# Geometric attention blocks ahead of the standard ones in each chunk of a causal two-attention layer with a ternary feed-forward

## The reference

```python
q, k = rope(xn @ Wq), rope(xn @ Wk)          # 8 query heads, 2 key heads of 32 channels
v = xn @ Wv                                   # 2 value heads
out = softmax(causal(q @ k.T / sqrt(32))) @ v               # "standard"
qp, kp = q[..., :3] . dirs[h], k[..., :3] . dirs[h]         # one number per token and head
geo_out = softmax(causal(outer(qp, kp))) @ v                # "geometric"
out = out + head_scales[h] * (geo_out - out)
attention = out @ Wo

z = xn @ ternary(W_syn).T + b_syn             # 1024 hidden units
hidden = relu(z) kept where z is among the 102 largest of its token
ffn = layernorm(xn + hidden @ ternary(W_out).T + b_out)
```

## Time and profile before

| | |
|---|---|
| median of 3 runs | 785.08 us (782.65 to 787.91) |
| profiled execution, its own time | 785.15 us |
| its span | 783.4 us |
| PE busy | 703.4 us, 90% of the span |
| DVE, ACT, POOL busy | 495.6, 464.9, 262.5 us |
| mean granted clock of PE | 0.896 |

### The profile page before, as it was taken

How to read it: one execution, slowest core, us unless ns; L and a number is a source line. 1 busy time by engine, 2 the same in 40 slices (tenths; PEclk the granted TensorE clock), 3 DMA queues, 4 the chain that set the end, 5 groups by cost and what they waited for, 6 DMA issues and landing times. The chain is left out here.

```text
span 783.4 us, 12828 instructions
## 1 busy us (share of the span) xinstructions
PE 703.4 (90%) x4536; PEld 351.5 (45%) x4536; DVE 495.6 (63%) x1022; ACT 464.9 (59%) x789; POOL 262.5 (34%) x390
## 2 busy tenths in 40 slices
PE   2779889989999997999999997799999999989954
PEld 1445434455344344543344334544544455554434
DVE  3798498854675686266474648274575576856463
ACT  3354762058654611765554461688889888988930
POOL 5516562043214104331030102302433543343355
PEclk9876987589799975999999898899999999999986
DMA  8100000000000000000000000000000000000000
GB/s 234 63 1 4 7 2 7 0 3 1 1 8 1 1 1 2 1 5 6 1 1 1 1 2 1 10 1 8 8 8 8 8 8 15 8 8 8 2 0 28
DMA packets 12373, 9.41 MB, mean 12 GB/s; under 512 B 5713, under 2 KB 11729, under 8 KB 12306
## 3 DMA queue, kind: packets, MB, share of 16 engines
q1 hardware_dynamic: 12306, 8.55, 3.8%
HBM read 5.80 MB, written 2.10 MB: 10 GB/s over the span
## 5 line engine op out<-in xcount | busy, mean ns | idle before, releaser
L728 ACT ACTIVATE probs<-scores 128x1024 f32<-128x1024 f32 (+3 forms) x320 | 269.8, 893 | 153.9 <-PE acc L1208 56.3
L1208 PE MATMUL acc<-probs,v_nat 128*32 128x512 f32 (+3 forms) x1280 | 159.0, 570 | 6.1 <-POOL probs L606 5.8
L1208 PE MATMUL acc<-probs,ones_all 128*32 128x512 f32 (+3 forms) x1280 | 153.7, 553 | 0.0
L926 DVE TENSOR_REDUCE piece_max<-side 128x1 f32<-128x512 f32 x156 | 103.5, 686 | 73.9 <-PE side L1107 72.9
L606 POOL TENSOR_SCALAR_AFFINE_SELECT probs<-probs 128x256 f32<-128x256 f32 x128 | 57.9, 463 | 156.8 <-ACT probs L728 155.8
L1107 PE MATMUL side<-k_stack,q_stack 96*128 96x512 f32 (+3 forms) x232 | 93.5, 462 | 3.7 <-DVE piece_max L926 1.8
L1188 PE MATMUL scores<-q_stack,k_stack 98*128 98x512 f32 (+3 forms) x320 | 92.2, 398 | 2.4 <-ACT probs L728 2.4
L1208 PEld LDWEIGHTS acc<-probs,ones_all 128*32 128x32 f32 x1280 | 43.0, 115 | 82.9 <-issue 80.1
L1107 PEld LDWEIGHTS side<-k_stack,q_stack 96*128 96x128 f32 x232 | 42.1, 203 | 71.2 <-issue 45.6
L1188 PEld LDWEIGHTS scores<-q_stack,k_stack 98*128 98x128 f32 x320 | 55.3, 195 | 27.5 <-ACT probs L728 19.1
L641 POOL TENSOR_TENSOR xb<-xn,b_down 128x256 f32<-128x256 f32 x16 | 12.4, 776 | 147.8 <-DVE y_mv L1059 138.3
(11 more groups left out here) (144 smaller groups left out, 1105.9 us busy)
## 6 DMA issues: line engine op xcount, KB each, us to landing
res<-in_L_attn_x_dram SPq DMA_DIRECT2D x4, 512.0 KB, 9.2
out_dram<-res SPq DMA_DIRECT2D x16, 128.0 KB, 1.7
z_buf<-in_L_ffn_W_syn_dram SPq DMA_DIRECT2D x1, 1024.0 KB, 7.8
z_buf<-in_L_ffn_W_out_dram SPq DMA_DIRECT2D x1, 1024.0 KB, 4.9
k_geo<-geo_rows SPq DMA_DIRECT2D x24, 8.0 KB
q_geo<-geo_rows SPq DMA_DIRECT2D x24, 8.0 KB
w_qkv<-in_L_attn_Wq_dram SPq DMA_DIRECT2D x1, 256.0 KB, 4.4
tables<-in_cos_table_dram SPq DMA_DIRECT2D x1, 256.0 KB, 4.5
```

The costliest lines, as they stand in the source:

```text
L728: nc.scalar.activation(probs[:, slot % 2, pair, :, off:], scores[:, pair, :, off:], ACT.Exp, scale=ATT_SCALE if kind == 0 else 1.0).then_i ...
L926: free(nc.vector.tensor_reduce(piece_max[:, h, p:p + 1], pt, AX.X, ALU.max), ("S",) + a)
L1208: last = nc.tensor.matmul(acc[D * h:D * h + D, part, off:], lhs, probs[:, slot % 2, h // 2, h % 2, off:], start=first, stop=end)
```

## The change

In every chunk the slots now run geometric group 0, geometric group 1, standard group 0, standard group 1 (`KINDS`). The other edits follow from that. The first epilogue of a group is now the geometric one, so it fills `mixed`, and the standard one mixes: the same four POOL operations, with the roles of the two buffers exchanged. q_geo holds one chunk in place of two, so its memset covers half; geo_dma of chunk c waits until the geometric slots of chunk c-1 have been used. The wait of q_in is put on the last slot of chunk c-2, which is now a standard one.

```diff
+KINDS = ((1, 0), (1, 0), (1, 0), (1, 0))
...
-            wait = [("vs", c - 2, G - 1, 1, TPC * (c - 1) - 1)] if c >= 2 else []
+            wait = [("vs", c - 2, G - 1, 0, TPC * (c - 1) - 1)] if c >= 2 else []
...
         add("geo", "sp", 1, ("geo_dma", c), 8000, [("geo_top", c), ("geo_lo", c), ("geo_hi", c), ("fill",)]
-            + ([("vs", c - 2, G - 1, 1, TPC * (c - 1) - 1)] if c >= 2 else []))
+            + ([("vs", c - 1, G - 1, 1, TPC * c - 1)] if c >= 1 else []))
...
-    slots = [(c, g, kind, j) for c in range(NCH) for g in range(G) for kind in range(2) for j in range(TPC * (c + 1))]
-    epilogues = [(c, g, kind) for c in range(NCH) for g in range(G) for kind in range(2)]
+    slots = [(c, g, kind, j) for c in range(NCH) for kind in KINDS[c] for g in range(G) for j in range(TPC * (c + 1))]
+    epilogues = [(c, g, kind) for c in range(NCH) for kind in KINDS[c] for g in range(G)]
...
-        unit("o", 0, ("o", t), 860, [("mix", t // TPC, G - 1, 1)])
+        unit("o", 0, ("o", t), 860, [("mix", t // TPC, G - 1, KINDS[t // TPC][1])])
...
-        q_geo = sb("q_geo", [P, 2, G, CHUNK], F32R)
+        q_geo = sb("q_geo", [P, G, CHUNK], F32R)
...
-                    if c >= 2:
-
-                        sp.wait_ge(probs_used, acc_done[2 * G * (c - 1) - 1])
+                    if c >= 1:
+
+                        sp.wait_ge(probs_used, acc_done[epi_no[(c - 1, G - 1, 1)]])
...
-                    if kind == 0:
+                    if kind == KINDS[c][0]:
...
-                        link(nc.gpsimd.tensor_tensor(o_raw[:], o_raw[:], mixed[:, g], ALU.subtract))
-                        link(nc.gpsimd.tensor_scalar(o_raw[:], o_raw[:], scale_h[:, g:g + 1], None, ALU.mult))
-                        link(nc.gpsimd.tensor_tensor(mixed[:, g], o_raw[:], mixed[:, g], ALU.add))
+                        std, geo = (o_raw[:], mixed[:, g]) if kind == 0 else (mixed[:, g], o_raw[:])
+                        link(nc.gpsimd.tensor_tensor(geo, geo, std, ALU.subtract))
+                        link(nc.gpsimd.tensor_scalar(geo, geo, scale_h[:, g:g + 1], None, ALU.mult))
+                        link(nc.gpsimd.tensor_tensor(mixed[:, g], geo, std, ALU.add))
```

More of the change, by code:

```diff
@@ L165, in build_plan @@
         add("recip", "dve", 2, ("recip", c, g, kind), 3400, [("d_raw", c, g, kind), ("o_raw", c, g, kind)])
-        add("mix", "pool", 2, ("mix", c, g, kind), 1350 if kind == 0 else 5700,
-            [("recip", c, g, kind), ("late",)] + ([("unit", "o", TPC * c - 1)] if kind == 0 and c else []))
+        add("mix", "pool", 2, ("mix", c, g, kind), 1350 if kind == KINDS[c][0] else 5700,
+            [("recip", c, g, kind), ("late",)] + ([("unit", "o", TPC * c - 1)] if kind == KINDS[c][0] and c else []))
     for t in range(NT):
-        unit("o", 0, ("o", t), 860, [("mix", t // TPC, G - 1, 1)])
+        unit("o", 0, ("o", t), 860, [("mix", t // TPC, G - 1, KINDS[t // TPC][1])])
         add("o", "dve", 0, ("o_add", t), 430, [("unit", "o", t)], empties=("o", t))
@@ L500, in _ @@
                     c = key[1]
-                    b, cols = c % 2, slice(CHUNK * c, CHUNK * c + CHUNK)
+                    cols = slice(CHUNK * c, CHUNK * c + CHUNK)
                     sp.wait_ge(geo_ready, c + 1)
@@ L515, in _ @@
                             at = GROWS * g + r
-                            sp.dma_start(q_geo[at:at + 97:32, b, g, :].bitcast(F32), src.bitcast(F32)).then_inc(geo_in[c], 16)
+                            sp.dma_start(q_geo[at:at + 97:32, g, :].bitcast(F32), src.bitcast(F32)).then_inc(geo_in[c], 16)
                 if k == "w_next":
@@ L694, in _ @@
                     if c >= 2:
-                        act.wait_ge(probs_used, acc_done[2 * G * (c - 1) - 1])
+                        act.wait_ge(probs_used, acc_done[epi_no[(c - 2, G - 1, 0)]])
                     free(nc.scalar.copy(q_stack[0:STK, c % 2, 4 * half:4 * half + 4, col:col + P],
@@ L1192, in _ @@
                             last = nc.tensor.matmul(dst[:, off:], k_geo[rows, P * j:P * j + P],
-                                                    q_geo[rows, b, g, off:], start=True, stop=True)
+                                                    q_geo[rows, g, off:], start=True, stop=True)
                     last.then_inc(score_full, 1)
```

## The result

The changed kernel takes **840.27 us** (median of 4 runs, 839.75 to 842.42) against 785.05 us (782.65 to 787.91) for the kernel before, run on the same chip: a ratio of 1.0697, 95% interval 1.0671 to 1.0723. It is 55 us slower, where 11 us were forecast. The profiled execution took 842.42 us at a span of 840.7.

What follows compares the result with a forecast made beforehand. PE was taken as the bound over the whole run, though not everywhere. 487.5 + 66.4 - 41.5 + 5.0 - 0.9 = 516.5; plus 149.7, 666.2; plus 17.5 + 96.6 + 13.9, 794.2 span; plus 1.75, 796 us; range 774 to 815.

Steps and rivals of the forecast that it cites:

- Work added ahead of mT of chunk 3, +66.4: Up to mT of chunk 3, PE gets chunk 3's 32 geometric slots, counted as 29 at 2.29 us: +66.4 us.
- The holes give back 41.5: Three stretches (132 to 164, 280 to 316, 475 to 492) where PE loses 41.5 us; geometric slots fill them.
- less 5.0: Up to mT of chunk 3: imperfect filling, 4.4% of some 110 us of added and moved work, costs 5.0 us.
- the term put at nothing beside it: Chunk 0's four standard slots leave the setup of chunk 1; costed at nothing, as that setup is through earlier without them.
- the 530 that was to show that the holes weren't won: Sign of being wrong: mT of chunk 3, forecast at 516.5, comes after 530 us.
- mT of chunk 3 to the last slot, 149.7: Stage from mT of chunk 3 to the last vs: as now, less 2.1 for feed-forward; 149.7 us, bounds -5 and +10.
- Tail, 128.0: Behind the last slot, eight found instead of one, feed-forward alone: 17.5 + 96.6 + 13.9 us.
- The seven rounds: Tail, h_lo of tile 8 to h_lo of tile 15: 14.0 us each, 96.6 in all, bounds -19 and +1.
- The wait for fo: In each tail round DVE waits for fo: 3.9 us after h_lo less 3.1 of two pick steps, 0.8 us.
- The rule of the Trainium skill: DVE and POOL share ports as an exclusive lock; if POOL always held it, hide takes 1.87 us, sum 4 us higher.
- The first hole isn't won: Rival: DVE bounds 132 to 164, S of chunk 1 ends no earlier than now; 811 us; chance 0.18.
- The feed-forward doesn't wait: Rival: in the tail PE and ACT deliver before DVE asks, rounds of 11.3 us; 777 us; chance 0.15.

Runs made afterwards that it cites:

- e1: Changed kernel with chunk 0 alone back in its order of before (standard, geometric, group by group): 816.71 us, ratio 1.0396 to the kernel before.
- e7: Changed kernel with chunk 0 as one standard group, both geometric groups, then the second standard group: 825.14 us, ratio 1.0505 to the kernel before.
- e15: Changed kernel with both standard groups of chunk 0 ahead of both its geometric ones: 813.46 us, ratio 1.0372 to the kernel before.
- e9: Changed kernel with the second half of z put behind fo of three tiles before, for tiles 11 to 15: 839.39 us, ratio 1.0673 to the kernel before.
- e14: Changed kernel with two buffers for `work` alone, side banks as they are: 825.02 us, ratio 1.0512 to the kernel before.
- e3: Changed kernel with chunks 0 and 3 back in the order of before, chunks 1 and 2 geometric first: 787.66 us, ratio 1.0026 to the kernel before.
- e2: Changed kernel with chunk 3 alone back in its order of before: 797.42 us, ratio 1.0134 to the kernel before.
- e5: Changed kernel with z, hT, found and fo of the first eight feed-forward tiles ahead of chunk 3's S units: 783.53 us, ratio 0.9979 to the kernel before.
- e6: Changed kernel with chunk 0 as before, first eight feed-forward tiles ahead of chunk 3's S units, their pick and hide at rank 1 on DVE: 770.46 us, ratio 0.9809.
- e8: All chunks in the order of before, with the first eight feed-forward tiles ahead of chunk 3's S units: 805.92 us, ratio 1.0264 to the kernel before.

## Why the prediction was wrong

- **Work added ahead of mT of chunk 3, +66.4**: right, 67.7 measured.
- **"The holes give back 41.5", less 5.0: this is the step that failed**, and with it the term put at nothing beside it. The holes gave back 22.9 us, and the loss elsewhere grew by some 25, where the sum had 5.0 for it. So the loss went from 75.2 to 78.5 instead of to some 40, and mT of chunk 3 came 42.6 us after the forecast, past the 530 that was to show that the holes weren't won. One cause is shown by experiment; a second rests on a comparison of traces; a third is only seen.
 - *Chunk 0.* The prediction costed at nothing that its four standard slots leave their place beside the setup of chunk 1, "but without them that setup is through earlier". It was not: 98.17 and 98.54. The setup is a chain, not PE's work; the slots had used its gaps, and no geometric slot runs there before 87.3. Chunk 0 put back moves mT of chunk 3 by 25 of the 42.6 us (e1), and one standard group beside the setup does as much (e7). Some 10 of the 25 are seen beside the setup itself, where the 40 us lose 21.2 in the changed kernel and 10.6 in e7. Why the stages behind it lose less as well is not settled.
 - *The stretch behind an mT.* The holes of the earlier trace rows from 280 to 316 and from 475 to 492 reach over the mT at 300 and 487.5. The prediction counted the whole of them as won, but a geometric slot can only fill the part behind an mT if one is left by then. Chunk 2's were used up at 350.9, chunk 3's at 555.9, 3 to 4 us ahead of their mT. Of the 11.6 us that the second hole still loses, some 9 lie behind the mT, and where slots were left nothing was lost (e15). e15 differs in chunk 0 too, so no run kept slots back for this alone.
 - Short drops of the clock at group borders remain, seen and not tested.
- **mT of chunk 3 to the last slot, 149.7**: 144.8, just inside its bounds of -5 and +10.
- **Tail, 128.0**: 136.9. Its head was 17.1 (17.5 forecast; last vs at 703.8, first h_lo of tile 8 at 720.9), its end 13.4 (13.9). The seven rounds were mis-sized: 106.4 from h_lo to h_lo instead of 96.6, 15.2 each and not 14.0, beyond the bound of +1. The wait for fo was 1.6 us in the mean, not 0.8 (11.3 us in the seven rounds). z ahead of fo goes with that, but taking half of z from there brought next to nothing (e9). The sum had no term for the ring through `work`; with two buffers a round, hide to hide, took 13.0 and not 15.7 (e14). (Hide to hide the changed kernel has a mean of 15.7, since the four o fall into the first round.) The rule of the Trainium skill (page "SBUF — State Buffer", section "SBUF: two separate sides") that was weighed there is small here: the eight hides took 11.5 us in all, 1.3 more than at 1.28 each, and in the row above the one that took 1.60 ran while POOL was at y_out (to 747.65), which the prediction took to be through by then. (It was not through beside the hide of 1.28 us in the earlier trace rows either: there the hide began first, and POOL's step, begun at 747.11, took 1.89 us, where the next tile's took 1.23.)
- **The rivals.** "The first hole isn't won" named the right chunk, but the hole itself was won (3.6 us left of 15.3); the loss came ahead of it, beside the setup. None of the rivals covered a loss that moves. "The feed-forward doesn't wait" is out (15.2 a round, not 11.3); a second `work` takes off 2.7 us of that (e14).
- **What the sum hid.** It treated the rear as slots that cover a feed-forward. The runs speak for the opposite reading: the rear goes more by the feed-forward than by the slots. With 64 slots it took 295 to 311 us, with 48 (e15) 298, with 32 279 to 289 (the edits of the tail left aside), as long as the feed-forward of some fifteen tiles was in it. It begins at mT of chunk 3, and what delays that mT delays the end, though not one for one (e3 and e7). Moving 32 slots ahead of it cost 62.4 us in front and gave back 16.7 in the rear (e2 against the changed kernel). e5, e6 and e8 fit this from the other side. What sets the length of the rear within that range is open.

## What to carry to other kernels

Before filling a hole with work from elsewhere, ask of each stretch what the work does where it stands now: slots that look free to move may be the only cover of a chain whose length does not change. Reckon a hole in two halves, ahead of the event that ends it and behind, and check that filler is left for the second. And when one flow can only start at an event, price a change by that event, and move the flow's start together with the work.

## What was not expected of the hardware

A PE that the profile counts as busy may still be short of work. The earlier trace rows shows it in part (26.9 of 32 us busy at 0.62). In e6 it is plainer: from the last geometric slot of chunk 3 to its mT, S units run nearly alone:

```profile
561.00:612.00 51.00, 48.44 (x106) 24.77 (x99) 50.34 (x105) 2.57 (x6) 0.11 (x1) 0.54 0.00 0
```

PE shows 48.4 of 51 us busy, at a granted clock of 0.54; DVE is busy for 50.3 and is the bound. By the measure used above that is 26.2 us of work, so nearly half of the stretch is lost, and it is the clock column and DVE's that tell, not PE's.
